# A three-layer graph convolution on one core: one-hot matrices built by ScalarE instead of VectorE

## The reference

```python
def _gcn_norm(edge_index, n_nodes):
    ...
    deg = segment_sum(ones, dst)
    dinv = where(deg > 0, rsqrt(maximum(deg, 1.0)), 0.0)
    norm = dinv[src] * dinv[dst]
def _gcn_conv(x, W, b, src, dst, norm, n_nodes):
    xw = x @ W
    msg = xw[src] * norm[:, None]
    return segment_sum(msg, dst) + b
h = conv(conv(conv(x, W1, b1), W2, b2), W3, b3)
x = layernorm(x + h)          # eps 1e-5, no scale, no shift
```

## Time and profile before

| | us |
|---|---|
| median of 3 runs | 3510.13 |
| lowest, highest | 3508.68, 3517.03 |
| the profiled execution | 3509.13 |
| its span | 3507.1 |
| PE busy | 2637.4 (75%) |
| POOL busy | 2574.0 (73%) |
| VectorE (DVE) busy | 1133.2 (32%) |
| ScalarE (ACT) busy | 126.9 (4%) |

### The profile page before, as it was taken

How to read it: one execution, slowest core, us unless ns; L and a number is a source line. 1 busy time by engine, 2 the same in 40 slices (tenths; PEclk the granted TensorE clock), 3 DMA queues, 4 the chain that set the end, 5 groups by cost and what they waited for, 6 DMA issues and landing times.

```text
span 3507.1 us, 23852 instructions
## 1 busy us (share of the span) xinstructions
PE 2637.4 (75%) x6574; PEld 1095.7 (31%) x6574; DVE 1133.2 (32%) x2036; ACT 126.9 (4%) x222; POOL 2574.0 (73%) x2511
## 2 busy tenths in 40 slices
PE   7788888888888867777777777766777777777776
PEld 5233333333333322222222222222222222222222
DVE  7222222222222222222222222232434443443334
ACT  1000000000000000000000000000000000000000
POOL 0677777777777657777777777767777777777775
PEclk9999999999999989999999999998999999999998
DMA  8677777777777657777777777766777777777776
GB/s 292 200 211 208 209 207 207 207 204 207 210 207 206 194 154 212 209 209 210 210 208 206 209 208 206 207 193 194 220 216 222 220 219 220 219 223 218 221 213 180
DMA packets 243792, 736.23 MB, mean 210 GB/s; under 512 B 43286, under 2 KB 44946, under 8 KB 243664
## 3 DMA queue, kind: packets, MB, share of 16 engines
q0 software_dynamic: 199440, 653.68, 65.3%
q1 hardware_dynamic: 44224, 81.08, 6.3%
HBM read 683.39 MB, written 51.20 MB: 209 GB/s over the span
## 4 chain that ended last, share of the span: by engine, by line
POOL 48%; issue 14%; POOLq 1%; PE 1%; DMA 1%; DVE 0%; ACT 0%; DVEq 0%
POOL ring L386 48%; POOLq L386 1%; PE ps L549 1%; DMA y_dram<-acc 0%; DMA ring<-y_dram,src_idx 0%; PE ps L602 0%; DVE acc L879 0%; ACT acc L683 0%; DVEq L876 0%; DVE h_sb L901 0%; DVE ln L907 0%; DVE h_sb L905 0%; POOLq L77 0%; DVE row_sb L887 0%; DVE h_sb L887 0%
## 5 line engine op out<-in xcount | busy, mean ns | idle before, releaser
L386 POOL DMA_INDIRECT ring<-y_dram,src_idx x2493 | 2571.1, 1031 | 910.6 <-issue 758.9
L549 PE MATMUL ps<-ring,onehot 128*128 128x512 f32 x4986 | 2371.7, 622 | 829.3 <-DMA ring<-y_dram,src_idx 757.2
L549 PEld LDWEIGHTS ps<-ring,onehot 128*128 128x128 f32 x4986 | 938.4, 197 | 2226.8 <-issue 1792.8
L879 DVE SCALAR_TENSOR_TENSOR acc<-ps,mask,acc 128x512 f32 x624 | 439.8, 747 | 1291.5 <-PE ps L549 1171.5
L861 DVE TENSOR_TENSOR onehot<-place_iota,lo_f 128x512 f32<-128x512 f32 x624 | 428.8, 688 | 879.5 <-PE ps L549 879.5
L575 PE MATMUL ps<-w,w_sb 128*128 128x512 f32 x376 | 169.0, 592 | 0.0
L683 ACT ACTIVATE acc<-h_sb,dinv 128x512 f32<-128x512 f32 x96 | 69.3, 721 | 1488.8 <-DVE h_sb L887 1488.8
L575 PEld LDWEIGHTS ps<-w,w_sb 128*128 128x128 f32 x376 | 71.4, 190 | 89.9 <-issue 89.9
L887 DVE SCALAR_TENSOR_TENSOR h_sb<-ps,dinv,bias 128x512 f32<-128x512 f32 x48 | 36.0, 751 | 135.2 <-PE ps L575 128.9
L679 ACT ACTIVATE w_sb<-ps 128x512 f32<-128x512 f32 x47 | 28.1, 597 | 667.2 <-PE ps L559 667.2
L687 ACT ACTIVATE ln<-ln 128x1 f32<-128x1 f32 x49 | 9.9, 203 | 1123.2 <-DVE ln L913 1123.2
(11 more groups left out here) (105 smaller groups left out, 164.3 us busy)
## 6 DMA issues: line engine op xcount, KB each, us to landing
ring<-y_dram,src_idx POOLq DMA_INDIRECT x2493, 3.8
y_dram<-acc SPq DMA_DIRECT2D x96, 256.0 KB
acc<-in_x_dram SPq DMA_DIRECT2D x1, 12288.0 KB
y_dram<-acc SPq DMA_DIRECT2D x12, 1024.0 KB
w_sb<-in_x_dram SPq DMA_DIRECT2D x48, 256.0 KB, 4.7
out_dram<-row_sb SPq DMA_DIRECT2D x48, 256.0 KB
w_sb<-in_L_gnn_W_dram SPq DMA_DIRECT2D x1, 1024.0 KB
w<-in_L_gnn_W_dram SPq DMA_DIRECT2D x1, 1024.0 KB
```

The costliest lines, as they stand in the source:

```text
L386: pool.indirect_dma_start(ring[:, s, :], None, y_dram[layer], bass.IndirectOffsetOnAxis(ap=rows, axis=0), bounds_check=N - 1, oob_is_err=F ...
L549: mm = pe.matmul(ps[:, g % BANKS, :], onehot[:, r, k, :], ring[:, r * CPQ + k, :], start=(opens and k == 0), stop=(closes and k == chunks ...
L879: dve.scalar_tensor_tensor(out=rows, in0=ps[:, g % BANKS, :], scalar=mask[:, part, own:own + 1], in1=rows, op0=ALU.mult, op1=ALU.add).then ...
```

## The change

ScalarE builds the one-hots of the ordinary path. For each quad it computes, chunk by chunk, the absolute value of `lo_f` minus `place_iota` into PSUM bank 7 (four ACTIVATEs of 128 columns), waits for them by the new semaphore `far_ready`, and then writes the rectified 1 minus that bank into the quad's slot of `onehot` (one ACTIVATE of 512 columns). The values are whole numbers, so the result is 1 where they are equal and 0 elsewhere. VectorE's comparison, with its seven quads ahead of the first layer, goes away. ScalarE's loop is now by steps: each of a step's four refills waits for the sum of its quad, `keep_turned` stands after the second, and `scale_rows` or `std` after the fourth. The first seven quads are built after the weight copies. As bank 7 is taken, the second of the last two turned tiles goes to bank 6 and the first to bank 4, instead of banks 7 and 6.

```diff
-        LAST_TURN_BANK, LAST_PRODUCT_BANK = 6, 2
+        LAST_PRODUCT_BANK = 2
         GROUP_BANK = 4
+        FAR_BANK = 7
+        LAST_TURN_BANKS = (4, 6)
...
         def _(act):
+            act.wait_ge(consts_ready, CONSTS)
             act.wait_ge(edges_turned, 1)
...
-            def fast_tile(layer, t):
-                if layer == 0:
+            def stage_places(n):
+                c = CPQ * (n % LAYER_QUADS)
+                if n > 0:
+                    act.wait_ge(hot_ready, n)
+                for k in range(CPQ):
+                    act.activation(ps[:, FAR_BANK, k * P:(k + 1) * P], place_iota[:, :], ACT.Abs,
+                                   bias=lo_f[:, c + k:c + k + 1], scale=-1.0).then_inc(far_ready, 1)
+                act.wait_ge(far_ready, CPQ * (n + 1))
+                act.activation(onehot[:, n % RING_QUADS, :, :].rearrange("p c n -> p (c n)"), ps[:, FAR_BANK, :], ACT.Relu,
+                               bias=ones[:, 0:1], scale=-1.0).then_inc(hot_ready, 1)
+
+            def refill(n):
+                if n + RING_QUADS < ALL_QUADS:
+                    act.wait_ge(summed, n + 1)
+                    stage_places(n + RING_QUADS)
+
+            def fast_step(layer, i, t):
+                first = layer * LAYER_QUADS + i * QUADS
+                refill(first)
+                refill(first + 1)
+                if t is not None and layer == 0:
                     keep_turned(t)
-                if layer < LAYERS - 1:
-                    scale_rows(layer, t)
-                else:
-                    std(t)
+                refill(first + 2)
+                refill(first + 3)
+                if t is not None:
+                    if layer < LAYERS - 1:
+                        scale_rows(layer, t)
+                    else:
+                        std(t)
...
                 act.wait_ge(dinv_ready, 1)
+                act.wait_ge(groups_ready, 1)
+                for n in range(RING_QUADS):
+                    stage_places(n)
                 for layer in range(LAYERS):
-                    for t in range(LOOP_TILES):
-                        fast_tile(layer, t)
+                    for i in range(STEPS):
+                        fast_step(layer, i, TILE_AT[i])
                     last_tiles(layer)
...
-            def stage_places(n):
-                c = CPQ * (n % LAYER_QUADS)
-                dve.tensor_tensor(onehot[:, n % RING_QUADS, :, :], place_iota[:, :].unsqueeze(1).broadcast_to([P, CPQ, P]),
-                                  lo_f[:, c:c + CPQ].unsqueeze(2).broadcast_to([P, CPQ, P]),
-                                  ALU.is_equal).then_inc(hot_ready, 1)
-
             def finish_quad(n):
                 dve.wait_ge(summed, n + 1)
                 if n % 2 == 1:
                     add_group(n // 2)
-                if n + RING_QUADS < ALL_QUADS:
-                    stage_places(n + RING_QUADS)
...
-                for n in range(EARLY_QUADS):
-                    stage_places(n)
-                dve.wait_ge(w_copied, 2 * FB + 4)
-                for n in range(EARLY_QUADS, RING_QUADS):
-                    stage_places(n)
```

More of the change, by code:

```diff
@@ L178, in gcn_three_layers_resnorm @@
         ORDER_BANK, TURN_BANK, PRODUCT_BANK, DEG_BANK = 4, 4, 5, 7
-        LAST_TURN_BANK, LAST_PRODUCT_BANK = 6, 2
+        LAST_PRODUCT_BANK = 2
         GROUP_BANK = 4
+        FAR_BANK = 7
+        LAST_TURN_BANKS = (4, 6)
         turned = ps[:, :, :].rearrange("p b n -> p (b n)")
         consts_ready = sem("consts_ready")
+        far_ready = sem("far_ready")
         pads_ready = sem("pads_ready")
@@ L596, in last_tiles @@
                     for k in range(FB):
-                        mm = pe.transpose(ps[:, LAST_TURN_BANK + j, k * P:(k + 1) * P], rows[:, k * P:(k + 1) * P], ident[:, :])
+                        mm = pe.transpose(ps[:, LAST_TURN_BANKS[j], k * P:(k + 1) * P], rows[:, k * P:(k + 1) * P], ident[:, :])
                     mm.then_inc(tile_turned, 1)
@@ L710, in last_tiles @@
                         act.wait_ge(tile_turned, LOOP_TILES + k + 1)
-                        act.activation(last_turned[k], ps[:, LAST_TURN_BANK + k, :], ACT.Copy).then_inc(turn_copied, 1)
+                        act.activation(last_turned[k], ps[:, LAST_TURN_BANKS[k], :], ACT.Copy).then_inc(turn_copied, 1)
                 for k in range(2):
```

## The result

| | before | changed |
|---|---|---|
| median, us | 3510.9 | 3449.43 |
| lowest, highest | 3508.68, 3517.03 | 3445.67, 3453.22 |
| ratio | | 0.9822 (0.9803 to 0.9841) |
| profiled span, us | 3507.1 | 3443.9 |

The changed kernel is faster by 61.5 us, 1.8%, in four runs of each. The forecast was 3462 with a range of 3435 to 3484. Later comparisons gave another picture; they come with the experiments.

A forecast was written before the change was run, and what follows sets the result against it. POOL's back-to-back gathers were taken as the bound: 3509.1 us less 48.7 of holds plus 1 at the layer ends gave 3461.4, forecast as 3462 us, range 3435 to 3484.

The forecast's parts named there:

- What bounds the kernel: All three layers: POOL writes gathers back to back, 1.302 us each at best, and everything else follows.
- The cause of the 83 us: Gathers of all layers: VectorE instructions with both tensors in SBUF hold gathers starting under them, 83 us together.
- The sum: Holds over three layers: 83 us less 0.5, 15.8 and 18 us that stay, so 48.7 us less.
- the give-back: Layers 1 and 2: bias and layernorm additions, now starting where the comparison did, hold gathers; 15.8 and 18 us stay.
- it needn't move: Layer 1: the distance from a quad's last gather to the VectorE instruction after its sum keeps its 7.55 us median.
- ScalarE: Loops of all layers: building one-hots costs ScalarE 1.92 us per quad, covered by a lead of seven quads.
- The table loads: Layer 2: changes between Sqrt and Abs might each load a table, 1.28 us, two per step, still covered.
- The ends: Layer ends: the store of layer 1's last loop tile goes out later; +1 us, between 0 and +4.
- A: Rival, gathers: a sum's end lengthens them, or ScalarE holds them as well, so no gain; 3511 us; chance 4%.
- B: Rival, all layers: ScalarE becomes the bound and the kernel is slower, about 3733 us; chance 4%.
- C: Rival, layers 1 and 2: holds come back in full, only 28 to 31 us won, 3480 us; chance 10%.
- D: Rival, layers 1 and 2: starts drift out of the sensitive place, no holds stay, about 3432 us; chance 7%.

The follow-up runs named there:

- e5: The changed kernel unaltered, run again beside the kernel before on a later chip; 3786.6 us, ratio 1.0089 to the kernel before.
- e3: Kernel before, with VectorE's comparison put ahead of the group addition after each odd quad; 3787.2 us, ratio 1.0016 to the kernel before.
- e1: Kernel before, with VectorE's comparison reading place_iota from a copy in PSUM instead of SBUF; 3790.2 us, ratio 1.0044 to the kernel before.
- e2: Changed kernel, with VectorE also doing the old comparison from SBUF into a spare PSUM bank; 3817.5 us, ratio 1.0118 to the kernel before.
- e6: Kernel before, with place_iota, the bias of layers 1 and 2 and the layernorm's x read from PSUM in the loops; 3759.9 us, ratio 1.0024.
- e4: Kernel before, with each quad's comparison made by four tensor_scalar of 128 columns; 3792.1 us, ratio 1.0035 to the kernel before.
- e12: Kernel before without sums and VectorE's additions, comparing three times per quad with place_iota from SBUF; 3662.2 us, ratio 0.9763 to the kernel before.
- e9: The kernel of e3 (comparison ahead of the addition) run again on another chip; 3763.7 us, ratio 1.0008 to the kernel before.

## Why the prediction was right, point by point

- **What bounds the kernel.** Right for the chip of the profile. POOL waited for PE 0.3 us before and 0.6 after, and its 63.3 us less are the whole change of the span. It was not a property of the kernel alone: on a later chip the changed kernel (e5) has POOL waiting 369 us. Of the kernel before there are only times from those chips, no trace; e3, which differs from it by one order, has POOL waiting 286 us.
- **The cause of the 83 us.** Right, and shown: e1 takes one input away and 169 starts give no long gather, e2 puts the instruction back and 214 of 225 are long, e6 takes all such instructions away and the excess is zero. The evidence from L879 was stronger than I had it: 274 gathers, not 42, start under it with over 0.15 us of it left, and none is long. What I missed is that a tensor_scalar holds gathers too (e4, and L940 in e6); on the first chip it cost nothing that can be seen.
- **The sum.** 48.7 us of holds less forecast, 58.8 measured. Layer 0: 0.5 left forecast, 0.2 measured. Layer 1: 15.8 and 12.3. Layer 2: 18 and 11.9. The mis-sized term is the give-back, and its step is "it needn't move". The distance from the quad's last gather to the start of L908 was to stay at 7.43 to 7.7 us; of the 48 of the loop, about 20 did, and the rest lie between 7.9 and 12.7. In layer 2 it is 11 of 49. 0.26 us per event in layer 1 and 0.25 in layer 2 came out, not 0.33 and 0.34. The trace shows what moved the starts. The granted clock in layers 1 and 2 was 0.93 and 0.92 where it had been 0.95, and a quad of PE takes longer at the lower level. 22 of the 48 L908 had no stretch at that level within the 8 us before them: 21 started 7.39 to 7.66 us after the gather, and they held by 0.34 us on average, as forecast. The other 26 had one: all started at 7.93 us or later, and they held by 0.18. In the trace of before only 3 of the 48 had such a stretch. That the clock would fall more often in the changed kernel was in no term of mine, and why it did isn't shown. So the sum came out 10 us too small for a reason that I hadn't seen, and the forecast was right in spite of it.
- **ScalarE.** 1.92 us per quad forecast; from 1195.30 (the first L708 of a quad) to 1197.26 (the end of its L711) it is 1.96. The table loads that I had bounded didn't come: the trace has two, at 7.6 and 57.1 us, both ahead of the first gather, and none in the loops. VectorE's wait for ScalarE's root is 161.6 us over 49 tiles, 3.3 us each and not the 7 that I gave. The Trainium skill, "ScalarE: Activation LUTs", section "Table sets", has relu, copy and abs in every set; the trace agrees.
- **The ends.** +1 us forecast, -4.5 measured, of which 1.7 are PE's clock at one place and 1.9 an earlier first gather. Neither was forecast, and both are luck as far as the trace shows. At the end of layer 1 POOL's pause was 18.5 us after 18.7: the store beside two others, which I had priced at 1 us, cost nothing that can be seen.
- **The rivals.** A (no gain) and B (ScalarE as the bound) fell in the first comparison; C and D were the ends of the give-back, and it came out between the forecast and D. Yet on the later chips the result is A's and worse, by a mechanism that none of my rivals had: PE's sums come late, and POOL waits for them.
- **Two rules on contention.** The Trainium skill, "SBUF — State Buffer", section "Who interferes with whom", says that a VectorE instruction with two SBUF inputs contends with a GpSimd instruction that reads SBUF; e1, e2 and e6 agree. The probe that it reports there, in which tensor_tensor didn't stall DMA, doesn't carry over to these gathers, which read their indices from SBUF: 551 of 578 in e12 were held.

## What to carry to other kernels

Look at the spread of a descriptor-writing instruction's length, not only at its mean: 998 ns at the median and 1527 at most meant that something held it, and laying the other engines' timelines over the long ones named it in one look. Where GpSimd's indirect DMAs are the bound, keep VectorE's large two-input instructions to one tensor in SBUF (the other in PSUM, or the work on ScalarE); e1 does that with one copy and one changed operand, at the price of that copy. A tensor_scalar doesn't help as much (e4). And a saving on the bounding engine is worth its time only as long as that engine never waits: time it on more than one chip before it is believed.

## What the runs showed of the hardware that was not expected

- A gather is held by a two-input instruction that runs as it starts, until 0.12 us short of that instruction's end. In the trace of before this fits 330 of 342 such gathers to 0.03 us. An instruction that starts later holds nothing: 0 of 337 gathers there. The exceptions are in e3 and e9, where five gathers were held by a comparison that started 22 to 31 ns after them.
- Where such instructions follow each other without a gap, the hold can pass from one to the next. Three gathers of e12 were held so through 8 to 11 of them and took 5.67, 7.47 and 6.06 us; most others in the same place were let go after the first.
- A 128x512 tensor_tensor or scalar_tensor_tensor on VectorE with one tensor in PSUM takes as long as with both in SBUF (0.68 and 0.69 us) and holds nothing.
- A tensor_scalar with one tensor in SBUF holds a gather too: for 0.07 us on average at 128 columns (e4), for 0.12 to 0.24 at 512 columns (four gathers in e6).
- The same program took 3511 us in one comparison and 3752 to 3778 in four others. In the traces from those chips PE slows to one matmul in 2 us in stretches of 7 to 27 us, at the lower granted clock, and VectorE, ScalarE and in the end POOL wait for it.
